# Routed experts in chunks of 128 rows instead of 256, with the rows stationary, the tokens of a chunk found on chip, and an expert's weights in one transfer

## The reference, cut to what matters

```python
# L2_ffn: 2048 tokens, each to its best expert of 8, beside a shared expert
logits = x @ gate_w; top_id = argmax(logits); score = sigmoid(max(logits))
xs = x * score                                     # x is layer-normed, 256 wide
y_e = (silu(xs @ rt_gate[e]) * (xs @ rt_up[e])) @ rt_down[e]     # 256 -> 512 -> 256
out = shared_expert(x) + y of expert top_id
# L3_ffn: 2048 tokens, each to its two best experts of 8
t = rmsnorm(x, g2); vals, idx = top_k(softmax(t @ router_w), 2); w = vals / sum(vals)
out = x + sum over the two of w * ((silu(t @ w1[e]) * (t @ w3[e])) @ w2[e])
```

## Time and profile before

| | us |
|---|---|
| median of 3 runs | 3711.96 |
| the profiled execution | 3721.08 |
| its span, first to last instruction | 3719.8 |
| TensorE busy in it | 3289.5 (88%) |
| VectorE, ScalarE, Pool busy | 1948.3, 1158.2, 541.4 |
| mean granted TensorE clock | 0.936 of full |

### The profile page before, as it was taken

The page is one execution under the profiler, slowest core; times in us unless marked ns, Lnnn a source line. Parts: engine busy times, 40 slices in busy tenths (PEclk is TensorE's granted clock), DMA queues, the critical chain, the costliest instruction groups (busy, mean ns, idle before and its releaser), DMA issues. The chain is left out here.

```text
span 3719.8 us, 40435 instructions
## 1 busy us (share of the span) xinstructions
PE 3289.5 (88%) x15524; PEld 2431.6 (65%) x15524; DVE 1948.3 (52%) x3247; ACT 1158.2 (31%) x2185; POOL 541.4 (15%) x849
## 2 busy tenths in 40 slices
PE   7989899999999999988999968799588789945994
PEld 5668676677677677656666656569567445535994
DVE  5987786577568568431111178412367566640222
ACT  4433334533633542212111113111023355521220
POOL 1216101001000000110000000202300221114223
PEclk8999999999999999988999989799799789977997
DMA  5100100100100010021000000215300110113553
GB/s 145 32 1 1 48 1 12 37 23 1 48 23 1 12 36 1 1 102 54 12 23 23 1 0 1 74 57 185 99 17 1 40 43 28 31 39 134 181 182 121
DMA packets 111543, 173.85 MB, mean 47 GB/s; under 512 B 28175, under 2 KB 74297, under 8 KB 111097
## 3 DMA queue, kind: packets, MB, share of 16 engines
q1 hardware_dynamic: 89897, 97.33, 8.5%
q0 software_dynamic: 21456, 73.94, 5.8%
HBM read 139.06 MB, written 31.98 MB: 46 GB/s over the span
## 5 line engine op out<-in xcount | busy, mean ns | idle before, releaser
L394 PE MATMUL psum<-Vt,shared 128*128 128x256 f32 x2240 | 516.5, 386 | 26.1 <-ACT shared L555 12.0
L394 PEld LDWEIGHTS psum<-Vt,shared 128*128 128x128 f32 x2240 | 421.3, 192 | 104.4 <-issue 48.6
L417 PE MATMUL psum<-Kt,xnTt 128*128 128x512 f32 (+1 forms) x960 | 343.9, 508 | 0.5 <-ACT xnTt L500 0.5
L1853 DVE TENSOR_TENSOR prep<-psum,prep 128x256 f32<-128x256 f32 x156 | 66.3, 425 | 415.3 <-ACT prep L1835 415.3
L417 PEld LDWEIGHTS psum<-Kt,xnTt 128*128 128x128 f32 x960 | 179.4, 189 | 158.6 <-issue 153.4
L880 DVE SCALAR_TENSOR_TENSOR x<-psum,gates,x 128x256 f32<-128x256 f32 x128 | 53.1, 478 | 388.2 <-PE psum L841 388.2
L2584 DVE TENSOR_REDUCE row<-psum 128x1 f32<-128x128 f32 (+7 forms) x256 | 188.0, 754 | 124.8 <-PE psum L2332 122.6
L852 PE MATMUL psum<-shared,expert_w 128*128 128x512 f32 x512 | 243.4, 598 | 10.3 <-DVEq L216 10.3
L841 PEld LDWEIGHTS psum<-expert_w,prep 128*128 128x128 f32 x1024 | 194.6, 190 | 80.8 <-issue 60.5
L1200 PEld LDWEIGHTS psum<-expert_w,prep 128*128 128x128 f32 x1024 | 194.6, 190 | 77.7 <-issue 57.4
L841 PE MATMUL psum<-expert_w,prep 128*128 128x256 f32 x1024 | 241.7, 379 | 0.0
(11 more groups left out here) (362 smaller groups left out, 5440.0 us busy)
## 6 DMA issues: line engine op xcount, KB each, us to landing
inner<-L_sorted SPq DMA_DIRECT2D x39, 256.0 KB, 5.6
L_results<-inner SPq DMA_DIRECT2D x39, 256.0 KB, 2.9
expert_w<-in_L_xattn_Wf SPq DMA_DIRECT2D x16, 512.0 KB, 5.7
expert_w<-in_L_ffn_w SPq DMA_DIRECT2D x16, 512.0 KB, 4.5
L_sorted<-qTt SPq DMA_DIRECT2D x1, 6144.0 KB, 29.0
weights<-q_parts SPq DMA_DIRECT2D x32, 144.0 KB
weights<-k_parts SPq DMA_DIRECT2D x96, 48.0 KB
weights<-in_L_xattn_Wk SPq DMA_DIRECT2D x4, 1024.0 KB, 4.8
```

The costliest lines, as they stand in the source:

```text
L394: ins = pe.matmul(o_bank(t), probT[0:rows, t % 2, c, :], Vt[0:rows, t // TB, c, :], start=(c == 0), stop=(c == CH - 1))
L417: ins = pe.matmul(flat[:, par * 3 * BANK + at:par * 3 * BANK + at + cols], xnTt[:, par, k, :], Kt[:, t // TB, k, src:src + cols], start=(k ...
```

## The change

- A chunk has 128 rows, and there are at most 23 and 39 chunks. In a chunk's products the turned rows are stationary (four products of 512 columns into two banks); the 128 x 512 hidden values are computed in one silu and one multiply, turned by four transposes, and four products of 256 columns give the result.
- The sorted buffers are gone. The normed rows are stored once, by token, with two plain DMAs. For each chunk on-chip one-hot tables are multiplied by codes of the tokens (bf16 products, `pe_tokens`), which gives each row's token; Pool gathers 128 rows by token (`fetch_rows`) and scatters a chunk's results by token and choice. The results then come back with four or eight plain DMAs of 0.5 MB.
- The weights of an expert are joined on the host so that a partition's share is one row of 12 KB, and one indirect DMA of 1.5 MB fetches them, into one of four slots. A chunk whose slot already holds its expert (the expert of four chunks before is the same) gets an index out of bounds, and moves nothing.
- The arithmetic of places is shortened (sums over tiles by TensorE), its constant tables are made before the router's logits, and several barriers go: TensorE starts the shared expert of L2 without waiting for the places, and turns the tokens into chunks beside it. The weights of the next attention are loaded during L2's loop.
- In both narrow attentions the multiply by the inverse sum goes from VectorE to Pool (`pool_attention`); in n = 6 Pool's `pool_feed_root(0)` is put behind tile 8.
- The clearing of the sorted buffers is gone.

```diff
-    TOTALS = (15, 24)
-    AHEAD = 2
-    slots3 = (expert_w[:, 0:3072], weights[:, 0:3072], expert_w[:, 3072:6144])
+    TOTALS = (23, 39)
+    WSLOTS = 4
+    slots4 = (weights[:, 0:3072], weights[:, 3072:6144], expert_w[:, 0:3072], expert_w[:, 3072:6144])
...
+    def dve_places(dve, r, chosen):
...
+        then(dve, dve.tensor_tensor(same[:, WSLOTS:], expert_of[:, WSLOTS:], expert_of[:, 0:total - WSLOTS], ALU.is_equal))
+        then(dve, dve.tensor_scalar(expert_row, expert_of, float(P), partition, ALU.mult, ALU.add))
+        then(dve, dve.scalar_tensor_tensor(expert_row[:, WSLOTS:], same[:, WSLOTS:], float(4 * E * P), expert_row[:, WSLOTS:],
+                                           ALU.mult, ALU.add))
...
+    def dve_positions(dve, r, chosen):
...
+        dve.tensor_tensor(there, iota[:, 0:total].unsqueeze(1).to_broadcast([P, J, total]),
+                          hi.unsqueeze(2).to_broadcast([P, J, total]), ALU.is_equal).then_inc(hot_made, 1)
+        dve.wait_ge(hot_made, hots_before(r) + 1)
+        dve.tensor_tensor(codes[:, :, 0, :], there, code[:, 0:J].unsqueeze(2).to_broadcast([P, J, total]), ALU.mult)
+        for j in range(0, J, HOTS):
+            dve.tensor_tensor(hot[:, j:j + HOTS, :], iota16.unsqueeze(1).to_broadcast([P, HOTS, P]),
+                              lo16[:, j:j + HOTS].unsqueeze(2).to_broadcast([P, HOTS, P]), ALU.is_equal).then_inc(hot_made, 1)
...
+    def pool_routed(pool, r, x_rows, y_rows, experts):
...
         pool.wait_ge(places_made, 2 * r + 2)
+        for c in range(3):
+            fetch_weights(c)
+        pool.wait_ge(tokens_made, r + 1)
+        pool.wait_ge(rows_stored, 32 * (r + 1))
+        for c in range(3):
+            fetch_rows(c)
+        if r == 0:
+            pool.wait_ge(acc_added, ACCS_SHARED)
+        fetch_weights(3)
+        for c in range(total):
+            if c + 3 < total:
+                pool.wait_ge(rows_turned, base + c + 1)
+                fetch_rows(c + 3)
+            if c + 4 < total:
+                pool.wait_ge(routed_second, base + c + 1)
+                fetch_weights(c + 4)
+            pool.wait_ge(routed_copied, base + c + 1)
+            if c >= 1:
+                pool.wait_ge(results_sent[(c - 1) % 3], 16 * uses_before(r, (c - 1) % 3, c, 3))
+            pool.indirect_dma_start(y_rows, bass.IndirectOffsetOnAxis(result_row[:, c:c + 1], 0),
+                                    y_out[:, c % 3, :], None).then_inc(results_sent[c % 3], 16)
...
+        for c in range(total):
+            first(c)
+            if c + 1 < total:
+                turn_rows(c + 1)
+            if c >= 1:
+                second(c - 1)
+            turn_hid(c)
+        second(total - 1)
...
+    def pool_attention(pool, n, after=None):
+
+        for t in range(NT):
+            par = t % 2
+            Pb = prob[:, par, :].rearrange("p (h c) -> p h c", h=H)
+            pool.wait_ge(shares_made, NT * (n - 5) + t + 1)
+            pool.tensor_tensor(Pb, Pb, row[:, par, H:2 * H].unsqueeze(2).to_broadcast([P, H, S2]), ALU.mult).then_inc(weights_made, 1)
+            if after:
+                after(t)
```

More of the change, by code:

```diff
@@ L592, in dve_softmax @@
         dve.wait_ge(dve_step, vs())
+        if not divide:
+            dve.reciprocal(total, total).then_inc(shares_made, 1)
+            return
         dve.reciprocal(total, total).then_inc(dve_step, 1)
@@ L1765, in stored_before @@
-    def stored_before(r, s, n):
-        return sum(len(range(s, TOTALS[q], 2)) for q in range(r)) + len(range(s, n, 2))
+        pe.matmul(psum[:, 6, 2 * P:3 * P], both_flat, ones[:, :], start=True, stop=True).then_inc(counts_made, 1)
+        pe.wait_ge(counts_kept, r + 1)
+        pe.matmul(psum[:, 6, 0:P], earlier, both_flat, start=True, stop=False)
+        pe.matmul(psum[:, 6, 0:P], tile_counts, earlier_tiles, start=False, stop=True)
+        pe.matmul(psum[:, 6, P:P + E], tile_counts, of_expert, start=True, stop=True).then_inc(counts_made, 1)
@@ new lines, in build, with act_codes, pe_tokens @@
+    ROUND = 12582912.0
+    def act_codes(act, r):
+        there, codes = in_chunk(r)
+        act.wait_ge(hot_made, hots_before(r) + 1)
+        act.mul(codes[:, :, 1, :], there, partition).then_inc(codes_scaled, 1)
+    def pe_tokens(pe, r):
+        J, total = (r + 1) * NT, TOTALS[r]
+        codes = in_chunk(r)[1]
+        pe.wait_ge(codes_scaled, r + 1)
+        for j in range(J):
+            if j % HOTS == 0:
+                pe.wait_ge(hot_made, hots_before(r) + j // HOTS + 2)
+            ins = pe.matmul(psum[:, 7, 0:2 * total], hot[:, j, :], codes[:, j, :, :].rearrange("p n c -> p (n c)"),
+                            start=(j == 0), stop=(j == J - 1))
+        ins.then_inc(tokens_found, 1)
@@ L1802, in second @@
+        def second(c):
+            w = slots4[c % WSLOTS]
+            pe.wait_ge(hid_kept, base + c + 1)
+            if r == 0 and c == 0:
+                pe.wait_ge(acc_added, ACCS_SHARED)
+            if c >= 2:
                 pe.wait_ge(routed_copied, base + c - 1)
-            for t in range(2):
-                ins = pe.matmul(psum[:, 4 + par, t * D:(t + 1) * D], hidden[:, m % 4, t * P:(t + 1) * P],
-                                w[:, j, :], start=(j == 0 and t == 0), stop=(j == FC - 1), skip_group_check=True)
+            for j in range(FC):
+                at = 2 * KD * F + j * D
+                ins = pe.matmul(psum[:, 6 + c % 2, 0:D], chunk_hidT[:, c % 2, j * P:(j + 1) * P], w[:, at:at + D],
+                                start=(j == 0), stop=(j == FC - 1))
@@ L2938 @@
     arrays, aps = {}, {}
+    for name, parts in JOINED.items():
+        inputs[name] = joined(*(np.asarray(inputs.pop(part)) for part in parts))
     for name, value in inputs.items():
```

506 lines of the change are left out of this document (261 added, 245 removed).

## The result

The changed kernel takes 3535.42 us (median of 4 runs, 3534.64 to 3536.25) and the kernel before, beside it, 3714.51 (3711.72 to 3718.15): a ratio of 0.9517, 95% interval 0.9501 to 0.9534, or -179.1 us. The forecast was -168.7, 3543 in a range of 3500 to 3612.

A forecast was written before the change was run, and what follows sets the result against it. TensorE's instructions bound the two chunk loops, and it idles in five gaps; together 636 of 3720 us. L2 -56.0, L3 -110.2 and the attentions -2.5 make -168.7 off the median of 3711.96: 3543, range 3500 to 3612.

The forecast's parts named there:

- just under 5.9: Chunk loops: a loading chunk's 1.84 MB take 5.7 us at 321 GB/s, within TensorE's 5.9 us a chunk.
- strided weights: Old chunk loops: TensorE instructions cost 0.24 us with first weights taken at a stride, against 0.21 packed.
- two of its own signs: Chunk loops: TensorE busy over 97% of both; the forecast is wrong if TensorE waits there for rows or weights.
- The chain over two tiles: Attention n = 5: transposes through reciprocal and Pool's multiply take 18.5 us for two tiles, 9.3 each; -4 us in all.
- the first rows land near 3342 at any speed of the positions: Before L3's loop: three weight fetches fill the queue from 3325 to 3340, so the loop starts at 3343 to 3345.
- The backs: Stretches behind the routed loops: L2 from last product to next attention, -9.5 us; L3 from last product to end, -24.5.
- The 1.2 for the early load: Behind L2's barrier: Pool's root and zeroing hide most of the next attention's weight load, so loading early gains 1.2 us more.
- The queue does delay some of the loading chunks: Chunk loops: the transfer queue sets a period of 8.8 us in 35 loading chunks, adding 100 us: 3643; chance 0.13.
- The slow case: Chunk loops: a fetch with 12 KB rows takes 18.9 us, unpipelined, adding 455 us: 3998; chance 0.03.
- The skip skips: Chunk loops: its rival said all 62 chunks load, 27 of them costing 1 us more each: 3570; chance 0.03.
- More came out than I had summed: Rival: TensorE's whole wait in n = 5 goes and a chunk takes 5.7 us, -16 - 12: 3515; chance 0.10.
- the port rival: Both attentions: Pool loses 1.44 us a tile to VectorE's port lock, +17, and L3's rows come 3 later: 3565; chance 0.12.

## Why the prediction was right, and where it missed

It was right in its time and in what brings it: eight of the ten stages came within 2.5 us of their term.

- **The chunk loops.** Forecast 141.2 and 237.7 with a chunk of 5.9 and 3 us of queueing each; measured 141.4 (gap included) and 236.7, with 5.82 and 8.6 us of queueing together. The step that put the transfers "just under 5.9" held only just: with every chunk loading the mean was 6.09. That the "strided weights" made 0.24 us an instruction was right; they were worth 21 us by themselves. By two of its own signs the forecast stood on the edge: TensorE was busy for 96.4% of L2's loop (97.8% of L3's) where over 97% was asked, and it did wait for rows, in 11 intervals.
- **n = 5, -4 forecast, -9.1 measured.** The chain over two tiles was the right mechanism, and the mis-sized term is Pool's multiply. I scaled 2384 ns for 1024 columns, 2.33 ns a column; this one takes 1.82. The line I took is also no multiply, as I called it, but an addition, whose second operand is one row of 256 for all four tiles; here it is one value for 77 columns. Which of the two differences makes the price was not tried. The chain of 18.5 less 0.7 is 17.8, measured 17.98, and over 15 intervals that and the last tile make the 9. With the lower clock of other traces at its head the gain is 7.4.
- **Before the shared expert and in it, -7.5 forecast, -10.9 measured.** TensorE's first product came 4.5 us behind the router, not 5.5, and 16 token products took 0.56 us, not 2.
- **L3's gap, -46 forecast, -51.2 measured (-49.7 to the first product, which the forecast meant).** The tokens were ready when I had them (19.3 us behind the choice, 19.9 forecast). But the step "the first rows land near 3342 at any speed of the positions" failed: rows landed 3.6 us behind their issue, and with the third fetch behind them only 0.8 sooner. The queue was nearly empty, and the 5 us from the tokens to the landed rows were too much, as were the 1.3 to 3 for turn, copy and start (1.5).
- **The backs, -9.5 and -24.5 forecast, -8.7 and -25.7 measured.** The 20.7 for L2 was 20.95. The 1.2 for the early load was 0.
- **n = 6.** The forecast +1.5 and the difference of the traces, +1.4, agree by chance. From the first query product to the last weighing n = 6 grew by 5.8 us (164.7 to 170.5): up to 2.9 by the move, the rest at the head, where the granted clock was 0.75 after and 0.85 before. The latent steps, 4.4 shorter, hid most of it.

The rivals. The queue does delay some of the loading chunks, but that costs 8 us in all, not 100. The slow case is out: transfers of 12 KB rows ran at 302 GB/s in the mean. The skip skips, and is worth some 10 us, not the 27 its rival gave. More came out than I had summed, by one of the two routes that this rival named (n = 5) and by two others. Two small sums in the prediction do not come out: 17 and 3 us for the port rival make 3563, not 3565, and half of the queue's price in L2 is 26 us, not 22; the range would end at 3614.

The port. Its rival said that Pool's multiply would lose to VectorE, and it never did. But a lock of that kind is in the kernel, the other way round: VectorE's scaling ends with Pool's memset wherever they overlap, in the kernel before too. The 4.03 us issue of the earlier trace rows, which I took as a sign of the lock, says less than I made of it. Two issues before it ran beside the same additions and took 1.11 and 1.10. In 12 of 14 traces just one issue beside those additions was long (2.80 to 4.11 us, ending 0.8 to 0.9 behind the last addition), and in two none; what picks it out is open. The Trainium skill (SBUF — State Buffer, the two physically separate sides) says that the pair of ports goes to one engine for a whole instruction; the scaling (4.25, 3.17 and 2.21 us beside the memset, 0.32 alone) agrees. I had weighed that sentence for the multiply that the change adds, and not for a memset that was there already.

## What to carry to other kernels

Count the rows that a loop really works on before pricing its instructions: smaller chunks cost more for each row here (11.64 against 11.47 us for 256) and the two loops still became some 75 us shorter, by padding less. Where one engine issues every transfer of a loop, its issues, about 1.3 us each with the pause behind, are a budget of their own, beside the bytes. And when barriers or waits are moved, look at what now runs side by side on VectorE and Pool: here a long memset belongs where VectorE has no scaling or conversion from SBUF to SBUF to do.

## What the hardware showed beyond that

- A Pool memset of 128 x 4928 float32 (4.2 us) holds up VectorE's scaling of 128 x 256 from SBUF to SBUF until it ends: in all 27 overlaps of the 14 traces the scaling ended 0.14 to 0.15 us behind it. The statistics' aggregate (1.17 us) and copies out of PSUM were not held.
- Pool's multiply of 128 x 1232 with a broadcast operand takes 2.25 us in all 32 cases, within 4 ns.
- An indirect transfer in which every index is out of bounds still costs Pool 1.0 us to issue (27 of them in the changed kernel, 1.01 to 1.02 us).
- A weight load of a 128 x 128 piece whose columns are four apart takes 326 ns, a packed one 195.
